# Preparing delta, B and C in smaller pieces, with two sets of banks, in three of four selective-scan layers

## The reference

```python
x_dbl = einsum('bdl,ed->bel', u, x_proj_w)          # 6 rows for dt, 16 for B, 16 for C
dt, Bs, Cs = split(x_dbl, [6, 6 + 16])
delta = softplus(einsum('brl,dr->bdl', dt, dt_proj_w) + dt_bias)
# the scan, for each step: h = exp(delta * A) * h + (delta * u) * B ;  y = sum(h * C)
```

## Time and profile before

| what | value |
|---|---|
| time, median of 3 runs | 35231.98 us (35160.76 to 35288.79) |
| the profiled execution, its own time | 35258.12 us |
| its span, first to last instruction | 35256.3 us |
| mean granted TensorE clock | 0.777 |
| busy: PE, PEld, DVE, ACT, POOL | 75%, 24%, 71%, 43%, 62% |

### The profile page before, as it was taken

The page is one execution under the profiler, slowest core; times in us unless marked ns, Lnnn a source line. Parts: engine busy times, 40 slices in busy tenths (PEclk is TensorE's granted clock), DMA queues, the critical chain, the costliest instruction groups (busy, mean ns, idle before and its releaser), DMA issues. The chain is left out here.

```text
span 35256.3 us, 353348 instructions
## 1 busy us (share of the span) xinstructions
PE 26406.9 (75%) x100774; PEld 8372.0 (24%) x100774; DVE 24871.2 (71%) x15541; ACT 15127.5 (43%) x20404; POOL 21995.5 (62%) x9902
## 2 busy tenths in 40 slices
PE   7857888885547788888876668888873758888884
PEld 3422222221223322222223222222211322222221
DVE  1237999997322289999981269999983139999995
ACT  1044555553233345555511345555541245555551
POOL 0016999996000089999930149999980029999991
PEclk8857888887667778888867668888876768888887
DMA  1022122213212222221243221222124232122214
GB/s 67 10 116 77 40 48 47 48 42 102 80 67 96 97 52 48 48 47 40 47 151 122 105 87 43 44 47 45 42 61 159 94 110 44 43 47 48 47 42 147
DMA packets 928980, 2422.06 MB, mean 69 GB/s; under 512 B 113744, under 2 KB 331668, under 8 KB 919504
## 3 DMA queue, kind: packets, MB, share of 16 engines
q1 hardware_dynamic: 927000, 2398.76, 24.4%
HBM read 1375.34 MB, written 1023.05 MB: 68 GB/s over the span
## 5 line engine op out<-in xcount | busy, mean ns | idle before, releaser
L1086 POOL TENSOR_TENSOR scan_hc<-scan_bc,scan_h 128x1024 f32<-128x1024 f32 x6912 | 16089.6, 2352 | 716.1 <-DVE scan_h L1248 712.5
L1248 DVE TENSOR_TENSOR_SCAN scan_h<-scan_da,scan_state,scan_dbu 128x1024 f32<-128x1024 f32 x6912 | 15983.3, 2335 | 246.4 <-ACT scan_da L1138 237.8
L1169 PE MATMUL scan_da<-scan_dd,scan_ssel 32*128 32x512 f32 x27648 | 9456.1, 776 | 2807.7 <-DVE scan_h L1248 2610.9
L1138 ACT ACTIVATE scan_da<-scan_da,scan_a_cur 128x1024 f32<-128x1024 f32 x6912 | 7517.9, 1088 | 8291.5 <-PE scan_da L1169 8286.9
L1169 PE MATMUL scan_p_du<-scan_dd,scan_ssel 32*128 32x512 f32 x27648 | 9670.6, 781 | 657.9 <-DMA scan_bc<-bc_d 197.7
L1235 DVE TENSOR_TENSOR scan_dbu<-scan_p_du,scan_bc 128x1024 f32<-128x1024 f32 x4608 | 5553.9, 1205 | 1008.8 <-PE scan_p_du L1169 986.4
L1072 POOL TENSOR_TENSOR scan_dbu<-scan_bc,scan_dus 128x1024 f32<-128x1024 f32 x2304 | 5420.9, 2353 | 154.5 <-ACT scan_dus L1112 148.4
L1169 PEld LDWEIGHTS scan_da<-scan_dd,scan_ssel 32*128 32x128 f32 x27648 | 2562.4, 224 | 10345.9 <-DVE scan_h L1248 8310.3
L1186 PE MATMUL scan_p_y<-scan_hc,scan_rsel 128*32 128x512 f32 x27648 | 4930.3, 795 | 6.7 <-POOL scan_hc L1086 6.7
L1169 PEld LDWEIGHTS scan_p_du<-scan_dd,scan_ssel 32*128 32x128 f32 x27648 | 2491.8, 219 | 3817.4 <-DVE scan_dbu L1235 2937.0
L856 PE MATMUL prep_p_dt<-prep_dtv,prep_wdt 12*128 12x384 f32 x2304 | 1449.3, 789 | 1930.7 <-DVE prep_delta L914 1730.8
(11 more groups left out here) (202 smaller groups left out, 13865.8 us busy)
## 6 DMA issues: line engine op xcount, KB each, us to landing
scan_bc<-bc_d SPq DMA_DIRECT2D x576, 512.0 KB, 12.3
du_d<-prep_du SPq DMA_DIRECT2D x384, 576.0 KB, 2.8
delta_d<-prep_delta SPq DMA_DIRECT2D x384, 576.0 KB, 3.7
scan_dd<-delta_d SPq DMA_DIRECT2D x1152, 192.0 KB, 4.8
scan_dd<-du_d SPq DMA_DIRECT2D x1152, 192.0 KB, 6.6
y_d<-scan_y SPq DMA_DIRECT2D x576, 384.0 KB, 5.1
merge_y<-y_d SPq DMA_DIRECT2D x384, 576.0 KB, 3.8
xs_d<-proj_xs_o SPq DMA_DIRECT2D x96, 588.0 KB, 3.4
```

Of the source, the lines that this page charges most:

```text
L1086: nc.gpsimd.tensor_tensor(hc[:, u % HC_SLOTS, :], c, h[:, u % H_SLOTS, :], ALU.mult).then_inc(hc_ready, 1)
L1138: nc.scalar.activation(da[u % DELTA_BANKS][:], da[u % DELTA_BANKS][:], ACT.Exp, scale=a_cur[:, u // UNITS, u % UNITS:u % UNITS + 1]).then_ ...
L1169: return nc.tensor.matmul(dst[:, half * H:(half + 1) * H], ssel[rows, i, :], dd[rows, s, m, j, :], start=True, stop=True)
L1248: nc.vector.tensor_tensor_scan(h[:, v % H_SLOTS, :], da[v % DELTA_BANKS][:], dbu[:, v % DBU_SLOTS, :], state[:, v % UNITS:v % UNITS + 1], ...
```

## The change

`prepare` becomes two functions. `prepare_causal` is the old one, used by layer 1 alone. The new `prepare` serves layers 0, 2 and 3 (`u_d` in, no `useq_d` out) and works on 96 pieces of 384 steps of all three tiles:

- PSUM holds two one-bank `p_dbl` and two three-bank `p_dt`; `dtv` has 4 slots, `useq` and `delta` 3.
- PE's program is: projections of pieces 0 and 1, then for each piece its expansion and the projection of the piece two ahead. `wx` is 128 columns wide: the dt columns stand twice, at rows 64 and 96 of the result, and the expansion of tiles 0, 1, 2 reads rows 64, 96, 64.
- The bias comes as a 13th row of `wdt`, against a row of ones that ACT makes with an Identity with a bias operand in place of Copy. L907 becomes a one-step `min`, L914 a plain `max` of PSUM and SBUF.
- ACT works in pairs of pieces: Exp, Exp, Ln, Ln, then two takes of `p_dbl`. DVE: two maxima, two caps of the next pair, two products.
- The product is written over `useq` in place and stored from there; the `du` buffer is gone. A `useq` slot is refilled when its three stores have landed.
- Stores are of 128 x 3 x 384 elements (rows of 1536 bytes), where they were 128 x 1152 (4608 bytes). All loops are written out, and each grid tile has its own semaphore.

```diff
+        STEPS = ALL * PIECES
...
+        useq = ph.sb("useq", [P, SLOTS, TILES, DW])
...
+        dtv = ph.sb("dtv", [P, DTV_SLOTS, N])
+        sp_b = ph.sb("softplus", [P, 2, TILES, N])
+        delta = ph.sb("delta", [P, SLOTS, TILES, N])
+        p_dbl = [ph.ps(f"p_dbl{b}", [P, 512]) for b in range(2)]
+        p_dt = [ph.ps(f"p_dt{b}", [P, TILES, 512]) for b in range(2)]
+        loaded = ph.sem("loaded")
+        grid_loaded = [ph.sem(f"grid_loaded{m}") for m in range(TILES)]
...
+                    store_bc(v)
+                for v in range(STEPS):
+                    if v + 2 < STEPS:
+                        store_bc(v + 2)
+                    sp.wait_ge(du_ready, v + 1 + ONE)
+                    sp.dma_start(du_d[:, :, v * N:(v + 1) * N], piece(v)).then_inc(du_stored[v // PIECES % SLOTS], 16)
+                    if l == 0:
+                        sp.wait_ge(reset_done, v + 1 + ONE)
+                    sp.dma_start(delta_d[:, :, v * N:(v + 1) * N], delta[:, v % SLOTS]).then_inc(delta_stored[v % SLOTS], 16)
+                for b in range(DTV_SLOTS):
+                    sp.wait_ge(bc_stored[b], 16 * STEPS // DTV_SLOTS + ONE)
+                for b in range(SLOTS):
+                    sp.wait_ge(delta_stored[b], 16 * STEPS // SLOTS + ONE)
+                    sp.wait_ge(du_stored[b], 16 * PIECES * ((ALL - 1 - b) // SLOTS + 1) + ONE)
+            @block.gpsimd
+            def _(g):
+                for c in range(ALL):
+                    k, own = divmod(c, CHUNKS)
...
+                    for m in range(TILES):
+                        if c == 0:
+                            g.wait_ge(grid_loaded[m], 16 + ONE)
+                        for src, dst in walk_pairs(walks[k], own, grids[m], useq[:, c % SLOTS, m, :]):
+                            g.tensor_copy(dst, src).then_inc(useq_ready, 1)
+            @block.tensor
+            def _(t):
+                def project(v):
+                    if v % PIECES == 0:
+                        t.wait_ge(useq_ready, (v // PIECES + 1) * COPIES + ONE)
+                    t.wait_ge(dtv_ready, max(v - 1, 0) + ONE)
+                    for m in range(TILES):
+                        last = nc.tensor.matmul(p_dbl[v % 2][:, 0:N], wx[:, v // (CHUNKS * PIECES), m, :], piece(v)[:, m, :],
+                                                start=(m == 0), stop=(m == 2))
+                    last.then_inc(dbl_done, 1)
+                def expand(v):
+                    t.wait_ge(dtv_ready, v + 1 + ONE)
+                    t.wait_ge(delta_ready, max(v - 1, 0) + ONE)
+                    for m in range(TILES):
+                        q = DT_ROWS[m % 2]
+                        last = nc.tensor.matmul(p_dt[v % 2][:, m, 0:N], wdt[q:q + K, v // (CHUNKS * PIECES), m, :],
+                                                dtv[q:q + K, v % DTV_SLOTS, :], start=True, stop=True)
+                    last.then_inc(dt_done, 1)
+                t.wait_ge(loaded, 16 * 4 + ONE)
+                for v in range(2):
+                    project(v)
+                for v in range(STEPS):
+                    expand(v)
+                    if v + 2 < STEPS:
+                        project(v + 2)
+            @block.scalar
+            def _(a):
+                def take(v):
+                    a.wait_ge(dbl_done, v + 1 + ONE)
+                    a.wait_ge(dt_done, max(v - DTV_SLOTS + 1, 0) + ONE)
+                    a.wait_ge(bc_stored[v % DTV_SLOTS], 16 * (v // DTV_SLOTS) + ONE)
+                    nc.scalar.activation(dtv[:, v % DTV_SLOTS, :], p_dbl[v % 2][:, 0:N], ACT.Identity, bias=ones[:]).then_inc(dtv_ready, 1)
+                a.wait_ge(loaded, 16 * 4 + ONE)
+                for v in range(2):
+                    take(v)
+                for v in range(0, STEPS, 2):
+                    for b in range(2):
+                        a.wait_ge(capped, v + b + 1 + ONE)
+                        nc.scalar.activation(sp_b[:, b], sp_b[:, b], ACT.Exp).then_inc(exp_done, 1)
+                    for b in range(2):
+                        a.wait_ge(exp_done, v + b + 1 + ONE)
+                        nc.scalar.activation(sp_b[:, b], sp_b[:, b], ACT.Ln, bias=1.0).then_inc(log_done, 1)
+                    for b in range(2):
```

The vector engine's program, the call and the layouts:

```diff
+                        if v + b + 2 < STEPS:
+                            take(v + b + 2)
+            @block.vector
+            def _(d):
+                def cap(v):
+                    d.wait_ge(dt_done, v + 1 + ONE)
+                    d.wait_ge(delta_ready, max(v - 1, 0) + ONE)
+                    nc.vector.tensor_scalar(sp_b[:, v % 2], p_dt[v % 2][:, :, 0:N], 40.0, None, ALU.min).then_inc(capped, 1)
+                def softplus(v):
+                    d.wait_ge(log_done, v + 1 + ONE)
+                    d.wait_ge(delta_stored[v % SLOTS], 16 * (v // SLOTS) + ONE)
+                    nc.vector.tensor_tensor(delta[:, v % SLOTS], p_dt[v % 2][:, :, 0:N], sp_b[:, v % 2], ALU.max).then_inc(delta_ready, 1)
+                def times_u(v):
+                    d.wait_ge(delta_ready, v + 1 + ONE)
+                    nc.vector.tensor_tensor(piece(v), delta[:, v % SLOTS], piece(v), ALU.mult).then_inc(du_ready, 1)
+                def reset(v):
+                    first = -(v % PIECES) * N % WINDOW
+                    d.wait_ge(du_ready, v + 1 + ONE)
+                    nc.vector.memset(delta[:, v % SLOTS, :, first::WINDOW], RESET_DELTA).then_inc(reset_done, 1)
+                for b in range(2):
+                    cap(b)
+                for v in range(0, STEPS, 2):
+                    for b in range(2):
+                        softplus(v + b)
+                    for b in range(2):
+                        if v + b + 2 < STEPS:
+                            cap(v + b + 2)
+                    for b in range(2):
+                        times_u(v + b)
+                        if l == 0:
+                            reset(v + b)
...
         if l == 1:
-            prepare(nc, l, wl, xs_d, PADDED, delta_d, du_d, bc_d, useq_d)
+            prepare_causal(nc, l, wl, xs_d, PADDED, delta_d, du_d, bc_d, useq_d)
         else:
-            prepare(nc, l, wl, u_d, SIDE, delta_d, du_d, bc_d, None)
+            prepare(nc, l, wl, u_d, delta_d, du_d, bc_d)
...
+    ones = np.zeros((P, 1), np.float32)
+    for q in DT_ROWS:
+        ones[q + IMAGES * RANK] = 1
+    c["c_dt_ones"] = ones
...
+        if l != 1:
+            twice = np.zeros((P, DIRS, TILES, P), np.float32)
+            twice[:, :, :, 0:DBL_ROWS] = w[f"l{l}_wx"]
+            for q in DT_ROWS:
+                twice[:, :, :, q:q + IMAGES * RANK] = w[f"l{l}_wx"][:, :, :, BC_ROWS:]
+            w[f"l{l}_wx"] = twice
+            w[f"l{l}_wdt"] = np.concatenate([w[f"l{l}_wdt"], w.pop(f"l{l}_dtb").transpose(1, 2, 0)[None]], 0)
```

More of the change, by code:

```diff
@@ L692, in _, with prepare, piece, store_bc @@
                                                     ALU.add).then_inc(lerp, 1)
-def prepare(nc, l, w, map_d, map_cols, delta_d, du_d, bc_d, useq_d):
+DT_ROWS = (BC_ROWS, 96)
+def prepare(nc, l, w, map_d, delta_d, du_d, bc_d):
+    with Phase(nc, f"prep{l}") as ph:
+        DW = CHUNK
+        N = SUB
+        PIECES = DW // N
+        SLOTS = 3
+        DTV_SLOTS = 4
+        ALL = DIRS * CHUNKS
+        STEPS = ALL * PIECES
+        K = IMAGES * RANK + 1
+        grid = ph.sb("grid", [P, TILES, L])
+        useq = ph.sb("useq", [P, SLOTS, TILES, DW])
+        wx = ph.sb("wx", [P, DIRS, TILES, P])
+        wdt = ph.sb("wdt", [P, DIRS, TILES, P])
+        ones = ph.sb("ones", [P, 1])
+        dtv = ph.sb("dtv", [P, DTV_SLOTS, N])
[5 more added lines that the diff above has]
+        grid_loaded = [ph.sem(f"grid_loaded{m}") for m in range(TILES)]
+        useq_ready = ph.sem("useq_ready")
+        dbl_done = ph.sem("dbl_done")
+        dtv_ready = ph.sem("dtv_ready")
+        bc_stored = [ph.sem(f"bc_stored{b}") for b in range(DTV_SLOTS)]
+        dt_done = ph.sem("dt_done")
+        capped = ph.sem("capped")
+        exp_done = ph.sem("exp_done")
+        log_done = ph.sem("log_done")
+        delta_ready = ph.sem("delta_ready")
+        du_ready = ph.sem("du_ready")
+        reset_done = ph.sem("reset_done")
+        delta_stored = [ph.sem(f"delta_stored{b}") for b in range(SLOTS)]
+        du_stored = [ph.sem(f"du_stored{b}") for b in range(SLOTS)]
+        walks = WALKS[l]
+        COPIES = TILES * (2 if walks[0][0] == "window" or walks[0][2] == "snake" else 1)
+        grids = [grid[:, m, :].rearrange("p (r c) -> p r c", c=SIDE) for m in range(TILES)]
+        def piece(v):
+            c, n = divmod(v, PIECES)
+            return useq[:, c % SLOTS, :, n * N:(n + 1) * N]
+        with ph.block() as block:
+            @block.sync
+            def _(sp):
+                sp.dma_start(wx[:], w["wx"]).then_inc(loaded, 16)
+                sp.dma_start(ones[:], w["dt_ones"]).then_inc(loaded, 16)
+                for q in DT_ROWS:
+                    sp.dma_start(wdt[q:q + K], w["wdt"]).then_inc(loaded, 16)
+                for m in range(TILES):
```

(16 more changed lines are left out.)

## The result

| kernel | median | range |
|---|---|---|
| before | 35206.53 us (4 runs) | 35160.76 to 35288.79 |
| after | 34160.43 us (4 runs) | 34125.57 to 34228.08 |

The ratio is 0.9703, 95% interval 0.9678 to 0.9728: 1046 us faster, where 1009 were forecast. The profiled execution took 34125.57 us on its own clock (span 34123.6). The prediction of 34,220 us is 60 us above the median, and every value of the range of runs lies inside 33,820 to 34,580.

What follows compares the result with a forecast made beforehand. A chain of latencies bounds the preparation stage; at 15.9 us a pair of pieces, 336 us a layer and 1009 in three go, so 35258.1-1009-26 = 34,220 us, range 33,820 to 34,580.

Steps and rivals of the forecast that it cites:

- The bound: Preparation stage before the change: no engine full, a chain of latencies, the product at 11.47 us a piece.
- The path of a pair at the lower clock: New loop: ACT's takes, expansion, projection, second expansion, cap, Exp, load, Ln; 16.94 us a pair with PE at 1.2 GHz.
- T: The end of the first Ln of a pair of pieces, from which the pair's times are counted.
- The clock: PE in the new loop: each pair begins low, rises in three of four, 1.4 us each; 15.9 us a pair.
- The head: Start of the stage: the first Ln of the first pair ends 23.05 us after the first projection starts.
- my sum for the old start: Stage before the change: 20.2 us from first projection to first product and 1.28 for a table load, taken as 21.5.
- Two quadrants: PE's expansion from rows 64, 96, 64 is two matmuls long: 2.97 us to the cap at the lower clock, 1.68 upper.
- the rival: No overlap of the quadrants in PE's expansions: 2.56 us more a pair at the low clock, 34,740 us; chance 0.17.
- The mode switch: PE between expansion and projection: 0.27 us for each switch on the path, half at the upper clock.
- The stores: Delta stores land in 3 to 5 us; the second maximum waits 0.6 us for its slot, at no cost.
- The slower rival: Delta stores landing late make the kernel slower from 15 us on; with 16 it is 35,350 us; chance 0.03.
- The table loads: ACT in the preparation stage: two a pair, 96 a layer in place of 192, none charged before a take.

Runs made afterwards that it cites:

- the unpaired run: Changed kernel with ACT and DVE going piece by piece, a table load before every Exp and every Ln: 33708.19 us, 0.9580 of the kernel before.
- the second experiment: Changed kernel with only PE's program reordered, both expansions of a pair and then both projections: 33559.89 us, 0.9544 of the kernel before.
- the best version: Changed kernel with both expansions of a pair before both projections on PE, and four delta slots for three: 33374.37 us, 0.9478 of the kernel before.
- the new order: PE's program in the changed kernel with both expansions of a pair, then both projections; alone 33559.89 us, 0.9544 of the kernel before.
- in the first: Changed kernel with all three expansions of a piece reading dt rows 64 to 76, none row 96: 34370.04 us, 0.9768 of the kernel before.

## Why the prediction held, point by point

- **The bound.** A chain of latencies before, and a chain after. With one set of banks the chain over the maximum returned and 810 us with it; with two sets the path goes over PE's program order, and changing that order alone gave 560 us. Both paths were predicted from the rows of before, and both are shown by a run; the prediction put no price on either.
- **The path of a pair at the lower clock.** Forecast 16.94, measured 16.56. Four terms came as forecast: 2.85, 4.14, 2.96 (forecast 2.97), and Exp, load and Ln. Two were a little large. PE starts at T+1.58 and not at T+1.90: the second Ln ends 1.06 after the first and not 1.18, the take ends 0.46 after that and not 0.60, since each instruction starts about 0.1 before the one before it has ended, and PE follows 0.06 later and not 0.12. And the cap lasts 1.36, not 1.42, so Exp follows after 1.40.
- **The clock.** The mean was right by two errors that cancel. I took a rise in three pairs of four, worth 1.4 us each. The distances of the first maxima in layer 0 repeat 16.56, 16.56, 14.67 through the whole stage: the clock rises in every third pair, but there 1.89 us are saved, since the rise comes inside the first projection, which takes 3.62 in place of 4.14, and the second expansion's cap comes after 1.60:

```profile
2226.85 3.70 PE L796 MATMUL prep_p_dbl<-prep_useq,prep_wx 128*128 128x384 f32 x6
...
2230.47 1.55 PE L806 MATMUL prep_p_dt<-prep_dtv,prep_wdt 13*128 13x384 f32 x6
...
2232.07 1.36 DVE L847 TENSOR_SCALAR prep_softplus<-prep_p_dt 128x1152 f32<-128x1152 f32 x1 [3.75 <-PE prep_p_dt L806]
```

So the clock gives 0.63 a pair, not 1.04, the takes and caps give 0.38, and the sum is 15.93; the last pair, which has nothing left to project, took 12.23, and the mean is 15.85 against 15.9. That the mean came so close was luck; the path was right.
- **The head.** This is the term that was mis-sized. The first maximum comes 17.1 us after the first projection starts, not 23.05, since the clock was up when the first pieces were made: 1.48 from expansion to projection where I had 2.85. The first projection itself stands 39.9 us after the load of `wdt`, where 42.5 had been, because GpSimd copies each grid tile as it lands; I had costed that edit at nothing. Together 8.5 us a stage, 26 in three, of the 33 by which the stages gave more than the 1009 forecast; the pair's 15.85 for 15.9 over 47 pairs gives 7 more. Against that the last product comes 5.4, 5.3 and 5.3 us after the last T, not 4.4, since the second maximum waits for its store: 3 in three. Of the 3 that are left, 1 is in my sum for the old start: I had 21.5 us from the first projection to the first product, and the trace has 21.8.
- **Two quadrants.** The overlap was taken from the scan's four records and held for three matmuls of 13 rows. The price that I gave to the rival, 2.56 a pair, is right for a pair at the lower clock, as the one pair of 19.12 shows, but too high in the whole: with one quadrant the clock was up in the second half of nearly every pair, and 1.2 is left.
- **The mode switch.** 2.85 from expansion to projection is 2.58 for two matmuls' columns and 0.27 for the switch, and 4.14 is 3.87 and 0.27. Where two projections follow each other without a switch, at the start of the stage, the second starts 0.64 us after the last record of the first starts, the distance inside a projection, with nothing added. At the upper clock the switch is 0.20, where I had taken half of 0.27 (1.48 for 1.28 of columns). The Trainium skill, TensorEngine Tiling (Array Packing), Key Properties, has the drain without a price; here the trace agrees with it at 0.27 us per switch at the lower clock.
- **The stores.** Delta landed after 4.8 to 5.0 us in the medians of the three layers, at the end of the 3 to 5 that I gave, and after 6.7 at most; the wait on it was 1.4 us where I had said 0.6; off the path, as the fourth slot showed. The slower rival needed a landing of 15 us and never came near.
- **The table loads.** No load stands before a take; one before each pair of Exp and one before each pair of Ln. Of the two, only L836's lies on the path; L833's runs while DVE caps. Halving them by pairing gave nothing in this order of PE: the unpaired run, with a load for each, is some 430 us faster. I had not asked that question, the prediction's sum holds the pairing as given.
- **Copies and products.** In the changed kernel's layers 0 and 2 they do not meet, no product takes over 1.35 us, and the copies of a chunk in layer 0 keep their 3.73 or 6.77 (6.83 at most). In layer 3 they do: 8 of 96 products take 1.53 to 1.62, which the prediction had named as a sign of being wrong. It costs nothing that the times show, as layer 3 gained the same 347 us. The bound of one copy, 1.13, was too low in general: in layer 3, whose longer copies take 2.1 each, the second experiment's products took up to 3.36, 2.0 more.

The spans of the two profiled executions differ by 1133 us and the three stages by 1042. The other 91 lie in the scans, which the change leaves alone: the four of them took 22,255 us before and 22,162 after. They vary as much without a cause in the kernel. With the fourth delta slot, where the preparation is as long as in the changed kernel, they took 22,262, and a single scan took between 5,508 and 5,611 us over all runs. The medians, which differ by 1046, agree with the 1042 of the stages.

## What to carry to other kernels

Give every term of a chain its row, and then read the programs of the engines in order: what the second buffer set freed was handed to the next instruction in an in-order queue. Here the change gave 0.0297 of the 0.0522 that the best version has; the rest lay in the order of four calls and in one slot that is worthless until the order is right. Batching saved half of the table loads here and still lost, since the batch waits for its last member; try it both ways.

## What the runs showed of the hardware

- TensorE's granted clock moved with the order of the work. In the same 500 us of layer 0 it was 0.60 before the change and 0.58 after it, 0.61 with longer expansions, 0.64 with one set of banks, 0.70 unpaired, 0.74 and 0.80 in the new order. It was no higher after the change than before it, although PE was busy for 399 us of the 500 in place of 280. A shorter chain paid twice in the second experiment: its pair was expected at 13.6 us at the lower clock and took 11.39. Longer PE work cost less than its own length in the first: 1.2 us a pair for one quadrant where the two rows are 2.56.
- A product and GpSimd's copies hold each other up. A chunk of row walks is copied in 3.73 us and one of column walks in 6.77 when alone; in the unpaired version most took 4.87 and 7.97, about one copy more, and the product shown there 1.89 in place of 1.35. In the new order copies of column walks took up to 9.2. In the rows one of the two runs and the other's record lasts until it is done: in the second experiment a product that starts at 1965.01 lasts 2.46 us and ends 1.2 after the copy that was under way, at 1966.25, and the next copy lasts 2.36 in place of 1.13. A waiting product can be passed by more than one copy: the longest, in layer 2 of the one-quadrant run in the new order, took 4.97 us beside four copies. The Trainium skill, SBUF - State Buffer, Who interferes with whom, names this pair of engines; these runs agree and give it a size, up to 3.6 us for a product and 1.1 to 2.4 for the copies of a chunk.
